# Attention kernel on one core: weighing matmuls in 64x32 tiles with two accumulators summed by GpSimd, two score banks instead of three, and each score next to a maximum matmul

## The reference

```python
qkv = (h @ w_qkv + b_qkv).reshape(B, T, 3, NUM_HEADS, HEAD_DIM)
scores = jnp.einsum('bhqd,bhkd->bhqk', q, k) / np.sqrt(HEAD_DIM)
attn = jax.nn.softmax(scores, axis=-1)
out = jnp.einsum('bhqk,bhkd->bhqd', attn, v)
```

## Time and profile before

| | us |
|---|---|
| median of 3 runs (1145.79 to 1149.45) | 1147.62 |
| the profiled execution, as timed | 1145.52 |
| its span in the profile | 1143.4 |
| stage 2's scores and weighing, in the span | about 136 to 787 |
| TensorE matmul busy in the span | 1060.8 (93%) |
| VectorE busy | 999.8 (87%) |
| ScalarE busy | 808.7 (71%) |
| GpSimd busy | 244.2 (21%) |

### The profile page before, as it was taken

One profiled execution on the slowest core, in us unless ns is written; L12 is line 12 of the kernel. 1 busy time (PEld: TensorE's weight loads), 2 busy tenths in 40 slices (PEclk: granted clock), 3 DMA queues, 4 the chain that ended last, 5 costly groups with the idle time before them and its releaser, 6 DMA issues.

```text
span 1143.4 us, 22167 instructions
## 1 busy us (share of the span) xinstructions
PE 1060.8 (93%) x8566; PEld 578.9 (51%) x8566; DVE 999.8 (87%) x1475; ACT 808.7 (71%) x1654; POOL 244.2 (21%) x345
## 2 busy tenths in 40 slices
PE   5997799999999999999999999997899998899995
PEld 4885233333333333333333333334667765788984
DVE  7786999999999999999999999943499998579887
ACT  4462188888888888888888888884567686343443
POOL 6423300000000000000000000102254333665643
PEclk9898599999999999999999999999899998899998
DMA  8595404315413432440442240212134325634321
GB/s 273 151 320 196 56 12 68 61 29 76 68 29 59 68 51 39 76 66 24 66 68 45 44 74 21 93 44 60 51 110 145 108 89 163 198 85 135 103 75 55
DMA packets 87332, 101.55 MB, mean 89 GB/s; under 512 B 21884, under 2 KB 57212, under 8 KB 87228
## 3 DMA queue, kind: packets, MB, share of 16 engines
q1 hardware_dynamic: 86396, 98.56, 36.2%
q10 hardware_dynamic: 832, 1.58, 0.4%
HBM read 55.09 MB, written 43.88 MB: 87 GB/s over the span
## 4 chain that ended last, share of the span: by engine, by line
PE 74%; DVE 12%; issue 2%; ACT 1%; POOL 1%; DMA 1%; SPq 0%; PEldq 0%; DVEq 0%; ACTq 0%; POOLq 0%
PE ps_o L792 26%; PE ps_s L780 20%; PE ps_m L769 10%; PE p_a L1337 4%; DVE maxes L727 2%; PE p_p L1763 2%; DVE p_kv_c L1261 1%; PE p_t L1343 1%; PE p_a L1740 1%; DVE p_q_c L1261 1%; PE p_p L1409 1%; PE p_t L1688 1%; PE p_p L1686 1%; DVE zT_lo L2026 1%; DVE ln_stats L69 1%
## 5 line engine op out<-in xcount | busy, mean ns | idle before, releaser
L678 ACT ACTIVATE prob<-ps_s 128x512 f32<-128x512 f32 x1024 | 556.0, 597 | 119.9 <-PE ps_s L780 100.3
L727 DVE TENSOR_REDUCE maxes<-ps_m 128x2 f32<-128x1024 f32 x512 | 621.0, 1221 | 19.1 <-PE ps_m L769 14.0
L792 PE MATMUL ps_o<-prob,v_ones 128*32 128x256 f32 x4096 | 327.8, 392 | 7.7 <-issue 7.3
L780 PE MATMUL ps_s<-q_stack,k_stack 64*128 64x512 f32 x1024 | 261.5, 500 | 0.0
L769 PE MATMUL ps_m<-k_stack,q_stack 62*128 62x512 f32 x1024 | 217.5, 417 | 15.5 <-DVE maxes L727 11.7
L780 PEld LDWEIGHTS ps_s<-q_stack,k_stack 64*128 64x128 f32 x1024 | 99.2, 184 | 211.4 <-ACT prob L678 187.9
L792 PEld LDWEIGHTS ps_o<-prob,v_ones 128*32 128x32 f32 x4096 | 81.7, 108 | 196.3 <-ACT prob L678 99.5
L638 POOL COPY v_ones<-v_all 128x512 f32<-128x512 f32 x16 | 9.9, 617 | 531.5 <-PE ps_o L792 531.5
L769 PEld LDWEIGHTS ps_m<-k_stack,q_stack 62*128 62x128 f32 x1024 | 101.5, 193 | 28.9 <-DVE maxes L727 24.8
L405 ACT ACTIVATE p_parts<-ps_qk,cols 128x512 fp32r<-128x512 f32 x32 | 22.0, 688 | 37.9 <-PE ps_qk L450 32.0
L1409 PE MATMUL p_p<-p_hT,w_p 128*128 128x512 f32 x96 | 42.7, 594 | 2.6 <-ACT p_hT L1174 2.6
(11 more groups left out here) (301 smaller groups left out, 1533.9 us busy)
## 6 DMA issues: line engine op xcount, KB each, us to landing
qk_parts<-p_parts SPq DMA_DIRECT2D x32, 512.0 KB, 7.1
q_stack<-qk_parts SPq DMA_DIRECT2D x96, 128.0 KB, 4.7
k_stack<-qk_parts SPq DMA_DIRECT2D x96, 128.0 KB, 7.9
oT<-o_sb SPq DMA_DIRECT2D x32, 256.0 KB, 3.0
x_all<-in_x_dram SPq DMA_DIRECT2D x8, 512.0 KB, 10.4
heads<-oT SPq DMA_DIRECT2D x16, 256.0 KB
inverse<-inverse_sums SPq DMA_DIRECT2D x16, 256.0 KB
out_dram<-x_all SPq DMA_DIRECT2D x7, 512.0 KB, 3.4
```

What stands on the lines that cost most here:

```text
L678: act.activation(prob[at % P_RING][:, h], ps_s[:, (GH * at + h) % S_RING], ACT.Exp, scale=HD ** -0.5).then_inc(exp_done, 1)
L727: dve.tensor_reduce(maxes[:, qc, i // 2, i % 2], ps_m[:, i % M_PAIRS], AX.X, ALU.max).then_inc(m_taken, 1)
L780: pe.matmul(ps_s[:, (GH * (UNITS * slot + KT * qc + kt) + h) % S_RING], r32(k_st[slot][rows, pair, kt * P:(kt + 1) * P]), r32(q_st[slot][r ...
L792: ins = pe.matmul(ps_o[32 * h:32 * h + 32, queries], v_st[slot][:, kt, h], prob[(UNITS * slot + KT * qc + kt) % P_RING][:, h, queries], st ...
```

## The change

- `weigh` splits the 128 keys into two halves of 64. Each head's product becomes two, of 64 keys x 32 columns, the lower keys into one bank and the upper keys into another (`ps_o` has two banks). Eight tiles of the array take part instead of four; the profile's count of instructions for it doubles.
- `take_o` copies both banks (1024 columns) to `o_parts`, and waits until the sum of the half before has been made. GpSimd adds the two halves to `o_sb` (`sum_o`), and `store` waits for that sum. The sums are woven into GpSimd's list: two ahead of each `place_v`, and the last ones between the divisions and ahead of `inverse_deviation`.
- `S_RING` is 2: a score waits for the exponential of the score two before it.
- TensorE's order in a pair is score, maximum matmul, score, maximum matmul, `weigh`. The maximum matmuls come in swapped order, so that each has the other parity than its score. The wait for the reduction stands before the first of the two, the signal on the second.

```diff
-S_RING = 3
+S_RING = 2
...
+        o_parts = sb("o_parts", [P, 2, CHUNK])
...
-        ps_o = ctx.enter_context(nc.psum_tensor("ps_o", [P, CHUNK], F32))
+        ps_o = ctx.enter_context(nc.psum_tensor("ps_o", [P, 2, CHUNK], F32))
...
             def store(g, qc):
-                sp.wait_ge(o_taken, QC * g + qc + 1)
+                sp.wait_ge(o_summed, QC * g + qc + 1)
...
+            def sum_o(g, qc):
+                pool.wait_ge(o_taken, QC * g + qc + 1)
+                pool.wait_ge(o_out[qc], 16 * g)
+                pool.tensor_tensor(o_sb[qc][:], o_parts[:, 0], o_parts[:, 1], ALU.add).then_inc(o_summed, 1)
...
-            for it in range(1, 5):
-                for u in range(3):
-                    place_v(3 * it + u, u)
-            place_v(NG - 1, 0)
+            for g in range(SLOTS, NG):
+                for qc in range(QC):
+                    sum_o(g - SLOTS, qc)
+                place_v(g, g % SLOTS)
+            for qc in range(QC):
+                sum_o(NG - 3, qc)
...
+            sum_o(NG - 2, 0)
             divide_heads(pool, heads, 0)
             divide_heads(pool, heads, 1)
+            sum_o(NG - 2, 1)
+            sum_o(NG - 1, 0)
             pool.wait_ge(var_ready, 1)
             inverse_deviation(pool, Steps(pool, dev_steps), rows_1["mv"][:, 0, 0, :, 1], const, rows_1["tmp"][:, 0, 0], rows_1["rstd"][:, 0, 0], rstd_ready)
+            sum_o(NG - 1, 1)
             divide_heads(pool, heads, 2)
...
             def take_o(g, qc):
                 act.wait_ge(pv_done, UNITS * g + KT * (qc + 1) + 2)
-                act.wait_ge(o_out[qc], 16 * g)
-                act.activation(o_sb[qc][:], ps_o[:], ACT.Copy).then_inc(o_taken, 1)
+                act.wait_ge(o_summed, QC * g + qc)
+                act.activation(o_parts[:], ps_o[:], ACT.Copy).then_inc(o_taken, 1)
...
-                if i % 2 == 0 and not (isinstance(n, int) and n < M_PAIRS):
+                if i % 2 and n >= M_PAIRS:
                     pe.wait_ge(m_taken, n - M_PAIRS + 1)
...
-                if i % 2:
+                if i % 2 == 0:
                     ins.then_inc(m_ready, 1)
...
                 for h in range(GH):
-                    ins = pe.matmul(ps_o[32 * h:32 * h + 32, queries], v_st[slot][:, kt, h],
-                                    prob[(UNITS * slot + KT * qc + kt) % P_RING][:, h, queries],
-                                    start=kt == 0 and half == 0, stop=kt == KT - 1 and half == 1)
+                    for part, keys in enumerate((slice(0, P // 2), slice(P // 2, P))):
+                        ins = pe.matmul(ps_o[32 * h:32 * h + 32, part, queries], v_st[slot][keys, kt, h],
+                                        prob[(UNITS * slot + KT * qc + kt) % P_RING][keys, h, queries],
+                                        start=kt == 0 and half == 0, stop=kt == KT - 1 and half == 1)
...
-                    for i in range(2):
-                        score_for_max(*to, i0 + 2 * pair + i)
+                    score_for_max(*to, i0 + (j ^ 1))
...
                         for pair in range(2):
-                            score(g, u, qc, kt, 2 * pair)
-                            score(g, u, qc, kt, 2 * pair + 1)
-                            scores_ahead(g, u, qc, kt, pair, last)
+                            for h in (2 * pair, 2 * pair + 1):
+                                score(g, u, qc, kt, h)
+                                score_ahead(g, u, qc, kt, h, last)
```

## The result

| | before | after |
|---|---|---|
| median, us | 1147.5 | 1232.4 |
| profiled span, us | 1143.4 | 1229.9 |
| TensorE instructions (matmuls) | 8566 | 12662 |
| VectorE busy | 87% | 82% |

The changed kernel is slower by 7.4%: the ratio is 1.074 (95% interval 1.0721 to 1.0758). The forecast was 1227 us, with a range of 1168 to 1250. For the profiled execution alone it was 1225, and 1232.0 was measured.

A forecast was written before the change was run, and what follows sets the result against it. TensorE's own sequence was taken as the bound, 1.24 us per pair. Pairs +68, last group +4, copy +5 and end +2 made +79 on 1145.5, 1225; the median, 2.1 higher, gives 1227 us, range 1168 to 1250.

The forecast's parts named there:

- The pair: Attention core: with two score banks a pair takes 1.38 us instead of 1.24, +68 us over 486 pairs.
- the held load: TensorE: the second score's weight load waits for an exponential to free its bank, starting 0.30 us into the pair, not 0.11.
- the loop itself: Two score banks: bank free at 1.68 us, plus 1.09 us from there to the next pair, over two: 1.38 us.
- That no gain comes from the change of tile shape: Weighing in eight tiles: the 0.38 us per pair around streaming stays, since a change of columns alone already costs 0.10 us.
- the first rival: TensorE: shape changes become free with all tiles 64 rows deep and loads go ahead; 1136 us, faster; chance 0.12.
- The skew of eight tiles: Weighing: four more tiles start 0.03 us later, at 0.007 us each, so weighing takes 0.57 to 0.60 us.
- The copy: ScalarE at each half's end: copying both banks loses 0.48 us per half instead of 0.32, 31 times, +5 us.
- The order: TensorE's pair: swapping scores and maximum matmuls costs nothing; with both scores at the pair's start a pair would take 1.68 us.
- GpSimd and the store: GpSimd's sum, 1.28 us per half, and the later store are hidden: 0; at the stage's end +2 us.
- The last group: Attention core's last group: 16 pairs with only scores and weighing go from 1.12 to 1.38 us, +4 us.
- an unheld second score: Rival, two score banks: exponentials come earlier than placed, so the second score does not wait; 1170 us; chance 0.05.
- tiles that run four at a time: Rival, weighing: the eight tiles don't run together, so weighing takes 0.43 us more; about 1325 us; chance 0.05.

The follow-up runs named there:

- the two runs on the copy: The changed kernel with ScalarE copying one bank only: 1217.6 us; the kernel before with its copy made 1024 columns long: 1161.9 us.

## Why the prediction was right

The forecast was +79 us on the profiled execution; its span grew by 86.5. By the steps of the sum:

- **The pair.** 1.38 us was said, 1.375 measured, and the alternation too. Its parts were less exact than their sum. From the held load to the weighing it takes 0.43 us in one pair (405.03 to 405.46) and 0.48 in the next (406.24 to 406.72), 0.455 in the mean, not the 0.49 that I took from the one case in the earlier trace rows; the weighing in eight tiles 0.59, not 0.60; and the held load may start 1.68 us after the pair's start in one pair, but 1.74 in every other one, 1.71 in the mean. There the first exponential of a tile starts 0.60 us after its load (406.05 to 406.65) instead of 0.54. The trace of the kernel before has the same alternation of 0.54 and 0.60; the earlier trace rows show only a pair of the first kind. It fits that ScalarE has one more wait at each new tile (`pv_done`, line 686), which I had not priced, but no run tests that. With the measured parts T = (1.71 + 0.455 + 0.59) / 2 = 1.38. The errors, +0.03, -0.035 and -0.01 us, cancelled, so that the hundredth was met is partly luck; the loop itself is what the runs bear out.
- **That no gain comes from the change of tile shape.** Right: weighing to the next score is 0.59 us, not the 0.43 of the first rival. The price of a change of columns alone in the earlier trace rows held for 64x32 as well. The trace agrees with the Trainium skill (TensorEngine Tiling (Array Packing), "Key Properties"), which has the array drained at each change of mode.
- **The skew of eight tiles.** 0.03 us was said, 0.02 measured (0.57 to 0.59); the medians in the trace's nanoseconds are 569 and 593, so 0.024. The 4 ns per tile of the Trainium skill (TensorE: Matmul & The Clock Gate, "Measured speedup vs the span model") would make 0.016 of it, my 7 ns 0.028. The starts inside one weighing are 6 to 7 ns apart in both kernels, which speaks for the 7.
- **The copy.** 0.48 us per half in place of 0.32 was said, 0.52 measured. The reason that I gave was half wrong. I had the extra columns partly absorbed by the wait for banks; the two runs on the copy show that they cost 14 and 15 us, and that the absorbed part is the old stall, of which 0.10 of 0.32 us are left. What the sum needed was the difference: 0.42 more (22.52 against 22.10) less 0.22, so 0.20 us per half, and the 0.16 said was near it.
- **The order.** It costs nothing (1148.5 us). But that both scores at the pair's start would give 1.68 us was a slip: I let the second score's wait hold the next pair whole, and did not use the loop that stands just above it. It gives 1.475, and 1.48 was measured.
- **GpSimd and the store.** Hidden, as said. At the end +2 was said and the span behind the last copy grew by 2.5 us (356.9 to 359.4). But the same stretch took from 356.9 to 363.4 us in the kernels of this study, most of which don't change it, so the total can't confirm that term.
- **What is missing.** The instruction gaps (5 us) have no term in the sum, nor has the start: the first reduction came 1.7 us later, within what the kernels of this study show there (103.3 to 106.9 us). The last group took 5.5 us more against 4 said, the first half 3.2 more.

The regular part of the halves is 29 x 2.37 = 69 us; with 5 of gaps, 3 in the first half, 5.5 in the last group, 2.5 at the end and 1.8 at the start the 86.5 us are whole.

Of the rivals, a free change of shape and loads made ahead don't appear in any timeline; an unheld second score appears only where the exponentials were shortened or the bank given back; and tiles that run four at a time would have shown a weighing near 1.0 us.

## What to carry to other kernels

A ring of buffers between two engines is priced by one loop: when the consumer frees the buffer, counted from the start of a period, plus what the producer has queued behind the held instruction, divided by the number of periods the loop spans. Write that sum down before taking a buffer away for something else; here it gave the period within 0.01 us from a few rows of the old trace, with errors of up to 0.035 us in the parts that cancelled. And before reshaping matmuls to avoid a switch, look for a switch in the trace that changes only the dimension that would still change.

## What the runs showed of the hardware

Splitting matmuls without changing what they stream made TensorE stop now and then: with 8192 weighing instructions instead of 4096 about a third of the halves are longer, the longest single gap being 1.89 us, where the kernel before has three halves longer by 0.25 us and no gap over 0.5 (between 160 and 740 us). The 16 gaps over 0.65 us in the kernels with the doubled count end 1.3 to 1.6 us after an instruction packet has come in. A reduction of 512 columns takes 0.68 us where one of 1024 takes 1.22. Two of them for one, with three banks for the maxima instead of four, cost 13 us in 512 pairs; the two parts were not separated.

In the unheld frame eight tiles of 64x32 over two banks run together: 16 instructions in 0.66 us, against 8 in 0.64 for four tiles of 128x32. Half the rows bring no speed by themselves.
